# Fills in pieces, stores waited for later in attention, and two buffers of spread sums at the output stage

## The reference, cut to what matters

```python
def longformer_mask(n):           # allowed: |i - j| <= 64, or i == 0, or j == 0
    ...
def attention(x):                 # 8 batches, 16 heads of 16
    Q, K, V = (split_heads(x @ W + b) for W, b in ((Wq, bq), (Wk, bk), (Wv, bv)))
    p = softmax(einsum('bhqd,bhkd->bhqk', Q, K) * 0.25 + mask)
    return merge(einsum('bhqk,bhkd->bhqd', p, V)) @ Wo + bo
def ffn(h):                       # 4096 tokens, 16 experts, each takes its 512 best tokens
    scores = softmax(h @ gate_w.T).T
    w, idx = top_k(scores, 512)
    g, u = h[idx] @ Wg.T, h[idx] @ Wu.T
    out = zeros.at[idx].add((gelu(g) * u) @ Wd.T * w)
    return out + (gelu(h @ Sg.T) * (h @ Su.T)) @ Sd.T
x = x + attention(layernorm(x))
x = x + ffn(layernorm(x))
```

## Time and profile before

| what | us |
|---|---|
| median of 3 runs | 1283.11 |
| the profiled execution | 1284.79 |
| its span, first to last instruction | 1282.8 |
| TensorE busy | 1158.4 (90%) |
| VectorE, GpSimd, ScalarE busy | 854.4, 630.6, 597.9 |
| first transposes of TensorE | 28.4 |
| attention's first instruction | 117.8 |
| output stage's first load | 441.3 |
| experts' stage, first to last | 698 to 1282.8 |
| granted clock of TensorE, mean | 0.955 of full speed |

### The profile page before, as it was taken

How to read it: one execution, slowest core, us unless ns; L and a number is a source line. 1 busy time by engine, 2 the same in 40 slices (tenths; PEclk the granted TensorE clock), 3 DMA queues, 4 the chain that set the end, 5 groups by cost and what they waited for, 6 DMA issues and landing times. The chain is left out here.

```text
span 1282.8 us, 23570 instructions
## 1 busy us (share of the span) xinstructions
PE 1158.4 (90%) x8906; PEld 969.1 (76%) x8906; DVE 854.4 (67%) x2182; ACT 597.9 (47%) x961; POOL 630.6 (49%) x792
## 2 busy tenths in 40 slices
PE   0997799989999549999985999999999999999997
PEld 0885577766677349987874788888888888888886
DVE  7895677767777057747876766666677666766641
ACT  1341466656666425432222555545455555545442
POOL 8000356656565426411001476666666676677654
PEclk9997699989999868999997999999999999999999
DMA  2589477777775376210132444444444444444311
GB/s 92 183 292 133 151 119 126 129 128 131 129 122 97 90 189 191 66 54 34 35 114 80 150 120 111 132 106 109 132 129 125 125 104 127 103 127 127 92 29 17
DMA packets 63053, 149.08 MB, mean 116 GB/s; under 512 B 15168, under 2 KB 32064, under 8 KB 53728
## 3 DMA queue, kind: packets, MB, share of 16 engines
q1 hardware_dynamic: 50592, 130.71, 39.3%
q0 software_dynamic: 12352, 16.92, 7.8%
HBM read 104.73 MB, written 42.34 MB: 115 GB/s over the span
## 5 line engine op out<-in xcount | busy, mean ns | idle before, releaser
L611 DVE CUSTOM_DVE_ANT_0 junk_s<-ps_s,mask 128x258 bf16<-128x258 f32 (+2 forms) x512 | 212.6, 470 | 91.8 <-PE ps_s L692 91.0
L1852 POOL TENSOR_TENSOR held<-h,held 128x512 fp32r<-128x512 f32 x128 | 178.4, 1406 | 124.0 <-ACT held L1888 123.8
L665 ACT ACTIVATE pt<-ps_p 128x516 f32<-128x516 f32 (+2 forms) x256 | 167.1, 680 | 82.0 <-PE ps_p L713 67.6
L1962 PE MATMUL ps_gu<-xt_hi,w_hi 128*128 128x512 f32 x512 | 203.3, 397 | 2.1 <-DVE xt_lo L1911 2.1
L1962 PE MATMUL ps_gu<-xt_lo,w_hi 128*128 128x512 f32 x512 | 200.2, 391 | 0.0
L1962 PE MATMUL ps_gu<-xt_hi,w_lo 128*128 128x512 f32 x512 | 200.0, 391 | 0.0
L1927 DVE TENSOR_TENSOR h<-ge,ps_gu 128x512 f32<-128x512 f32 x128 | 87.9, 686 | 165.1 <-ACT ge L1882 141.1
L1790 DVE TENSOR_TENSOR w_lo<-w,w_hi 128x768 fp32r<-128x768 f32 x128 | 174.7, 1369 | 31.1 <-ACT w_hi L1785 27.6
L498 POOL TENSOR_SCALAR_AFFINE_SELECT pt<-pt 128x256 f32<-128x256 f32 x352 | 133.0, 417 | 119.8 <-ACT pt L665 119.6
L1979 PE MATMUL ps_y<-w_hi,held 128*128 128x256 f32 x1024 | 187.9, 282 | 3.4 <-ACT stage L1898 1.7
L692 PE MATMUL ps_s<-ks,qs 96*128 96x258 f32 (+2 forms) x512 | 157.3, 364 | 9.3 <-PEq L198 9.1
(11 more groups left out here) (198 smaller groups left out, 2140.5 us busy)
## 6 DMA issues: line engine op xcount, KB each, us to landing
w<-in_We SPq DMA_DIRECT2D x48, 1024.0 KB, 4.9
qk_parts<-held SPq DMA_DIRECT2D x8, 2064.0 KB, 7.8
qs<-qk_parts SPq DMA_DIRECT2D x96, 129.0 KB, 4.2
ks<-qk_parts SPq DMA_DIRECT2D x96, 129.0 KB, 5.6
x<-in_x SPq DMA_DIRECT2D x16, 512.0 KB, 7.9
attn_t<-on SPq DMA_DIRECT2D x32, 256.0 KB, 5.9
ot<-attn_t SPq DMA_DIRECT2D x16, 256.0 KB, 4.6
rd<-rden SPq DMA_DIRECT2D x16, 256.0 KB, 4.1
```

What stands on the lines that cost most here:

```text
L611: dve.tensor_tensor_reduce(junk[:, (u * SG + g) % RING, 0:n], ps_s[:, (u * SG + g) % RING, 0:n], m, 1.0, -3e38, ALU.add, ALU.max, mx[:, u ...
L665: act.activation(dst, src, ACT.Exp, scale=SCALE).then_inc(exp_s, 1)
L1852: pool.tensor_tensor(h_lo[:, m], h32[:, (e * KI + m) % HB], h_hi[:, m].bitcast(F32), ALU.subtract).then_inc(hlo_s, 1)
L1962: last = pe.matmul(ps_gu[:, m % 2, n], l, r, start=c == 0, stop=c == 3 * KD - 1)
```

## The change

1. Projection: instead of three memsets ahead of the loop, GpSimd fills one place of `qs` (zeros) and of `ks` (ones, all rows) at a time: place 0 first, places 1 to 4 in steps 1 to 4 behind a wait for `xn_s`. The casts of mask and identity move to step 5. SP waits for the ten memsets before it loads the places.
2. The store of projection's last batch is issued as attention's first DMA, behind the barrier.
3. Attention: `store_rden(b)` moves from step 3 of batch b+1 to step 0 of batch b+2 and no longer waits for its store; `load_den` waits for it instead. The wait at the end for attention's stores goes to the output stage, ahead of the load of the last sums.
4. ScalarE does `far_rows(u + 1)` behind the seventh exponential, ahead of `out_rows`, instead of behind the sixth.
5. Output stage: `rd` becomes two buffers (the second is the tile `xg`, not yet used). Loads go in the order rd 0, ot 0, x 0, rd 1, ot 1, x 1, wait for attention's stores, sums, x 2 and so on. The load of rd b waits for division b-2.

```diff
-                sp.wait_ge(ready, 4)
+                sp.wait_ge(fill_s, 2 * SL)
                 for u in range(SL):
                     sp.wait_ge(out_s[u // UB % 2], (u // UB // 2 + 1) * 16)
                     load_step(sp, d, ks, qs, qk_in, u)
                 step(B // 2 - 1, 0, False)
-                step(B // 2 - 1, 1, False)
...
-                pool.memset(qs[:].bitcast(F32), 0.0).then_inc(ready, 1)
-                pool.wait_ge(ready, 2)
-                pool.memset(ks[:].bitcast(F32), 0.0).then_inc(ready, 1)
-                pool.wait_ge(ready, 3)
-                pool.memset(ks[M_ROW:M_ROW + 2].bitcast(F32), 1.0).then_inc(ready, 1)
...
+                def fill(place):
+                    pool.memset(qs[:, place].bitcast(F32), 0.0).then_inc(fill_s, 1)
+                    pool.memset(ks[:, place].bitcast(F32), 1.0).then_inc(fill_s, 1)
+                fill(0)
                 for b in range(B):
+                    if 1 <= b < SL:
+                        pool.wait_ge(xn_s, b + 1)
+                        fill(b)
+                    if b == SL:
+                        pool.wait_ge(m_in, 16)
+                        pool.tensor_copy(mask[:], m32[:]).then_inc(ready, 1)
+                        pool.wait_ge(i_in, 16)
+                        pool.tensor_copy(ident16[:], ident[:]).then_inc(ready, 1)
                     pool.wait_ge(qlo_s, b * 4 + 4)
...
                     for s in range(2):
                         sp.wait_ge(out_s[s], 16 * (UB // 2) * (b + 1))
+                    if b >= 1:
+                        sp.wait_ge(rden_out, b * 16)
...
                 def store_rden(b):
                     sp.wait_ge(rden_s, b + 1)
                     sp.dma_start(d["rden"][b].rearrange("h (c i) -> (h c) i", i=DC), den[:]).then_inc(rden_out, 16)
-                    sp.wait_ge(rden_out, b * 16 + 16)
...
+                sp.dma_start(d["qk"][B - 1].rearrange("c (m t) d h q -> (t d h) c m q", m=KD),
+                             qk[:, 1].rearrange("p c m k i -> p c m (k i)").bitcast(F32)).then_inc(qk_out[1], 16)
                 m_rows(0)
...
-                    if b >= 1 and t == 3:
-                        store_rden(b - 1)
+                    if b >= 2 and t == 0:
+                        store_rden(b - 2)
+                store_rden(B - 2)
                 store(NU - 2)
                 store(NU - 1)
+                sp.wait_ge(rden_out, (B - 1) * 16)
                 sp.wait_ge(bo_in, 16)
-                for h in range(2):
-                    sp.wait_ge(out_s[h], 16 * NU // 2)
...
+                        if n == 6 and u + 1 < NU:
+                            far_rows(u + 1)
                         if n == 6 and u >= 1:
                             out_rows(u - 1)
-                        if n == 5 and u + 1 < NU:
-                            far_rows(u + 1)
...
-        rd = sb("rd", [P, KD, S])
+        rd = [sb("rd", [P, KD, S])[:], lists.xg[:].rearrange("p c n -> p (c n)").rearrange("p (k q) -> p k q", k=KD)]
...
                 def load_rd(b):
-                    if b >= 1:
-                        sp.wait_ge(on_s, b)
+                    if b >= 2:
+                        sp.wait_ge(on_s, b - 1)
...
+                load_rd(0)
                 load_ot(0)
-                load_rd(0)
                 load_x(0)
+                load_rd(1)
                 load_ot(1)
                 load_x(1)
+                for h in range(2):
+                    sp.wait_ge(ot_out[h], 16 * NU // 2)
                 den_rows = d["ot"][B - 1].rearrange("t (h r) (c i) -> t h r c i", r=32, i=DC)[:, :, DH]
                 sp.dma_start(den[:], den_rows).then_inc(den_in, 16)
-                load_rd(1)
...
-                    dve.wait_ge(rd_in, (b + 1) * 32)
-                    dve.tensor_tensor(ot[:, b % 2], ot[:, b % 2], rd[:], ALU.mult).then_inc(on_s, 1)
+                    dve.wait_ge(rd_in[b % 2], (b // 2 + 1) * 16 * KD)
+                    dve.tensor_tensor(ot[:, b % 2], ot[:, b % 2], rd[b % 2], ALU.mult).then_inc(on_s, 1)
```

More of the change, by code:

```diff
@@ L122, in build, with mlp @@
         qk_out = [sem("p_out0"), sem("p_out1")]
+        ot_out = [sem("a_out0"), sem("a_out1")]
         project(nc, d, sem, tally, ident, bias, eps, ks, qs, v, mask, ident16, qk_in, qk, qk_out)
-        attend(nc, d, sem, tally, ks, qs, v, mask, ident16, qk_in, qk_out, held, stage)
+        attend(nc, d, sem, tally, ks, qs, v, mask, ident16, qk_in, qk, qk_out, held, stage, ot_out)
         att.close()
-        mlp(nc, d, sem, tally, ident, eps, held, stage)
-def mlp(nc, d, sem, tally, ident, eps, held, stage):
+        mlp(nc, d, sem, tally, ident, eps, held, stage, ot_out)
+def mlp(nc, d, sem, tally, ident, eps, held, stage, ot_out):
     TT = T // P
@@ L147, in mlp @@
         weights = ExpertWeights(nc, ctx, sem)
-        front(nc, d, sem, tally, ident, eps, group, wparts, pm, probs, seg, cur, blk, before, lists, weights, ht_b, held, stage)
+        front(nc, d, sem, tally, ident, eps, group, wparts, pm, probs, seg, cur, blk, before, lists, weights, ht_b, held, stage, ot_out)
         weights.place_parts(nc, ctx)
@@ L180, in project @@
         whi = sem("p_whi")
+        fill_s = sem("p_fill")
         ready = sem("p_ready")
@@ L233, in _ @@
                 pool.memset(eps[:], EPS).then_inc(ready, 1)
-                pool.wait_ge(ready, 1)
-                pool.memset(qs[:].bitcast(F32), 0.0).then_inc(ready, 1)
-                pool.wait_ge(ready, 2)
-                pool.memset(ks[:].bitcast(F32), 0.0).then_inc(ready, 1)
-                pool.wait_ge(ready, 3)
-                pool.memset(ks[M_ROW:M_ROW + 2].bitcast(F32), 1.0).then_inc(ready, 1)
-                pool.wait_ge(ready, 4)
-                pool.wait_ge(m_in, 16)
-                pool.tensor_copy(mask[:], m32[:]).then_inc(ready, 1)
-                pool.wait_ge(i_in, 16)
-                pool.tensor_copy(ident16[:], ident[:]).then_inc(ready, 1)
-                pool.wait_ge(ready, 6)
-                for b in range(B):
+                def fill(place):
+                    pool.memset(qs[:, place].bitcast(F32), 0.0).then_inc(fill_s, 1)
+                    pool.memset(ks[:, place].bitcast(F32), 1.0).then_inc(fill_s, 1)
+                fill(0)
+                for b in range(B):
+                    if 1 <= b < SL:
[6 more added lines that the diff above has]
+                        pool.tensor_copy(ident16[:], ident[:]).then_inc(ready, 1)
                     pool.wait_ge(qlo_s, b * 4 + 4)
@@ L417, in load_step, with attend @@
             sp.dma_start(dst[n * DH:(n + 1) * DH, u % SL].bitcast(F32), d["qk"][u // UB, part, u % UB]).then_inc(qk_in[u % SL], 16)
-def attend(nc, d, sem, tally, ks, qs, vs, mask, ident16, qk_in, qk_out, held, stage):
+def attend(nc, d, sem, tally, ks, qs, vs, mask, ident16, qk_in, qk, qk_out, held, stage, out_s):
     with ExitStack() as ctx:
@@ L801, in _, with front @@
                     times_v(NU - 1, i)
-def front(nc, d, sem, tally, ident, eps, group, wparts, pm, probs, seg_probs, cur, blk, before, lists, weights, ht_b, held, stage):
+def front(nc, d, sem, tally, ident, eps, group, wparts, pm, probs, seg_probs, cur, blk, before, lists, weights, ht_b, held, stage, ot_out):
     UG = UB // KD
@@ L876, in front @@
         ot_in = [sem("o_ot_in0"), sem("o_ot_in1")]
-        rd_in = sem("o_rd_in")
+        rd_in = [sem("o_rd_in0"), sem("o_rd_in1")]
         x_in = [sem(f"o_x_in{b}") for b in range(B)]
@@ L951, in load_rd @@
                 def load_rd(b):
-                    if b >= 1:
-                        sp.wait_ge(on_s, b)
+                    if b >= 2:
+                        sp.wait_ge(on_s, b - 1)
                     for k in range(KD):
-                        sp.dma_start(rd[:, k], d["rden"][b, k * (NH // KD):(k + 1) * (NH // KD), :].unsqueeze(0)
-                                     .to_broadcast([DH, NH // KD, S])).then_inc(rd_in, 16)
+                        sp.dma_start(rd[b % 2][:, k], d["rden"][b, k * (NH // KD):(k + 1) * (NH // KD), :].unsqueeze(0)
+                                     .to_broadcast([DH, NH // KD, S])).then_inc(rd_in[b % 2], 16)
                 def load_x(b):
```

1 line of the change is left out of this document (removed).

## The result

The changed kernel takes 1251.85 us (median of 4 runs, 1250.91 to 1253.89), the kernel before 1282.51 beside it (4 runs, 1281.70 to 1285.75). The ratio is 0.9758, 95% interval 0.9737 to 0.9780: 2.4% faster. The forecast was 1251.6. The profiled execution took 1251.19, its span is 1249.5.

What follows compares the result with a forecast made beforehand. TensorE in the expert stage bounds the kernel, so gains only shift that stage's start. 19.1 + 0 + 10.7 + 1.7 = 31.5 us off 1284.79 gives 1253.3, less 1.7 to the median: 1251.6; range 1243.5 to 1261.

Steps and rivals of the forecast that it cites:

- Fills: Projection: with small memsets the first xn is no longer held and all later work moves 19.1 us earlier.
- Last projection store: Seam of projection and attention: attention starts about 7.9 us earlier, but the rows of maxima do not; gain 0.
- Attention: Attention's steps: stores waited for later remove 11.5 us of excess, less 0.8 for ScalarE's new order; gain 10.7 us.
- The removable part: Attention: 11.5 of the 12.1 us by which 29 steps exceed 29 x 8.88, leaving 0.6 for VectorE's reciprocals.
- The 0.5 for transfers still late: Attention: 0.5 us taken off the gain for transfers that would still come late.
- The swap: ScalarE copies the rows of maxima behind the seventh exponential, not the sixth: 0.3 us lost, upper bound 6.
- End of attention: SP no longer waits for the last stores before the barrier; the output stage's first load goes 1.7 us earlier.
- Output stage: Output stage: exchanged load order makes no difference and the second buffer gives 0; at most 2.1 us lost.
- A: Projection loop: the small memsets hold VectorE, four steps 3.5 us longer, 1265.6 us; chance 0.07.
- B: Attention: late transfers come from the queue, not SP's waits; its gain falls to about 1, 1261.3 us; chance 0.16.
- C: Seam of projection and attention: rows of maxima land early and the 7.9 us are gained, 1243.7 us; chance 0.10.
- D: Projection: memset time does not follow row length, ten take 8.7 us each; slower, 1296 us; chance 0.02.

Runs made afterwards that it cites:

- experiment 1: The kernel before with only the fills in pieces, nothing else of the change: 1264.27 us, ratio 0.9837.
- Experiment 2: The changed kernel with all ten small memsets back to back ahead of the projection loop: 1258.28 us, ratio 0.9796.
- experiment 5: The changed kernel with projection's last store back ahead of the barrier: 1252.67 us, ratio 0.9761.
- the repeated run: The changed kernel run again without an edit: 1252.23 us, ratio 0.9767.
- experiment 4: The changed kernel with ScalarE's copy of the rows of maxima back behind the sixth exponential: 1251.08 us, ratio 0.9752.
- experiment 3: The changed kernel with the reciprocal sums' store and SP's wait for it back at their old place: 1259.82 us, ratio 0.9804.
- experiment 8: The changed kernel with the wait for attention's last stores back at attention's end: 1254.86 us, ratio 0.9779.
- experiments 7: The changed kernel with three places loaded in projection, and step 0's rows of maxima ahead of place 3, the last store and place 4: 1240.97 us, ratio 0.9666.
- experiment 11: The changed kernel with rows of maxima ahead, their copy behind the sixth exponential, projection's last store in four parts over steps 1 to 4: 1235.01 us, ratio 0.9636.

## Why the prediction was right

The forecast of 1251.6 stands 0.3 from the measured median. The mechanisms were right, but that it is so near is in part luck. At the output stage's first load the traces show 31.8 us for the 31.5 of the sum, but with 1.0 more at the seam and 0.8 less from there on; another 1.3 came behind that load, where nothing was forecast. So the two profiled executions lie 33.6 us apart (1253.3 was forecast, 1251.19 measured), and the medians 30.7.

- **Fills, 19.1 predicted.** 19.2 to 19.3 at three stations, and experiment 1 alone moves the first exponents' arguments by 20.2. The reading behind it was right: the xn instructions had been held by the memsets, two of the four by a whole one, the first by the rest of one, and the last hardly (2.05, 8.86, 8.86 and 0.97 us). The estimate of 1.75 to 1.95 for a piece met 1.82, and the margin to the next xn was there (1.19 us at 36.72). Experiment 2 gives the price of ignoring it.
- **Last projection store, 0 predicted.** Right by experiment 5: attention started 7.8 us later, ScalarE got its rows within 0.1 us of the same time. The first exponents' arguments came 0.9 us earlier than the fills explain in this trace; experiments 1 and 5, which have the store at its old place, have that too (121.24, 121.40), and the repeated run has 0.2 only. So it is not the store's; what it is stays open.
- **Attention, 10.7 predicted, 10.4 found.** The removable part was 11.5. The 0.5 for transfers still late was not needed: none was late. The swap was mis-sized: I put 0.3 for it, argued that it fits with 0.1 to spare, and it costs 0.04 in each step, 29 x 0.04 = 1.2 by the steps and 0.99 by experiment 4. Step 30, outside the 29, is 0.37 longer as well (7.95 for 7.58). That SP's standing still at this store was the cause is shown by experiment 3, which gives back 8.5 of the 10.4 when it alone returns. But the prediction priced only the landing, 2.9 us each time, and passed over the 8.3 us that SP waited for the reciprocals at the same place; the change removes both. Of the remaining 1.9, experiment 1 has 1.65 with the fills alone; the rest may be hidden by the swap, which experiment 3 keeps.
- **End of attention, 1.7 predicted.** 1.66 between the two traces from TensorE's last product to the first load, 1.68 by experiment 8.
- **Output stage, 0 predicted for the order and the second buffer.** The second buffer was read rightly: the division it frees starts 2.7 us nearer to the first product, and ScalarE's instruction behind it does not move. The order stays open within 1 us.
- **The rivals.** A (pieces hold VectorE in the loop): xn keeps 1.38 beside all pieces. B (the queue's own lateness): refuted by the changed kernel, which has the same loads and no late step, and by experiment 3; the late steps go with SP's waits. C (the seam gives its 7.9): refuted by experiment 5, because the rows pass nothing in the queue. But its upper bound was too small as a bound for the seam: experiments 7 and 11 show that 16 us lay there, for an order of the queue that this change does not make. D (memset time not by row length): 1.82 for 2064 elements, 8.70 for 10320.

## What to carry to other kernels

Ask of each late small transfer what stands before it in its issuer's program and in its queue: SP stood still some 2.9 us for a landing nobody needed yet and up to 1.9 for a reciprocal, and that cost up to 5.5 us of TensorE in one place; four small copies taken out from behind a 2 MB store and twelve loads brought attention's first step 16.7 us forward. Starting a stage earlier brings nothing while its first real input still stands behind the same transfers; put the small transfer first and spread the bulk over the steps behind it. Cut long GpSimd fills into pieces and place them right behind the VectorE operation they would hold.

## What the runs showed of the hardware that I had not expected

The output stage, from its first product to the start of the expert stage, has the same instructions in all these kernels, and took between 242.6 and 249.8 us. The first 120 us of it, for the changed kernel, its repetition, and experiment 1 (columns as in the window above):

```profile
421.99:541.99 120.00, 106.49 (x674) 97.94 (x675) 74.41 (x165) 49.78 (x60) 46.92 (x26) 0.87 0.42 124
```

```profile
421.55:541.55 120.00, 106.29 (x670) 97.86 (x671) 73.55 (x164) 49.77 (x60) 46.95 (x26) 0.85 0.43 125
```

```profile
430.90:550.90 120.00, 103.27 (x640) 94.80 (x641) 72.43 (x161) 47.85 (x58) 47.76 (x26) 0.86 0.44 126
```

The stage took 242.7, 243.4 and 249.8 us in these three, and the mean granted clock of the first 120 us does not order them: 0.85 goes with 243.4 and 0.86 with 249.8. A shorter stretch does show part of it. The 14 us that begin 118 us behind the first product, for the changed kernel and for experiment 1:

```profile
539.99:553.99 14.00, 12.67 (x66) 10.86 (x67) 9.13 (x24) 5.20 (x7) 6.59 (x6) 0.88 0.11 39
```

```profile
548.90:562.90 14.00, 14.00 (x63) 12.71 (x62) 4.80 (x10) 4.42 (x5) 1.26 (x1) 0.63 0.11 37
```

In experiment 1 TensorE is busy for all of the 14 us at 0.63, in the changed kernel for 12.67 at 0.88; 14 x (0.88 - 0.63) = 3.5 us of full speed less, by this estimate half of the 7.1 by which the stage is longer. Experiment 2, with a stage of 248.7, also has 0.63 there, and the repetition 0.88. What decides it I can't say: I made no experiment on it. It is why one profile of a kernel is not enough to settle a difference of 2 us behind this stage, while the 29 steps of attention repeated to 0.01 us in the two profiles of the changed kernel.

Windows 106 to 121 us of the changed kernel and of experiment 11, at the seam:

```profile
106.00:121.00 15.00, 0.00 (x0) 0.00 (x0) 0.75 (x5) 0.00 (x0) 0.21 (x1) 0.50 0.90 294
```

```profile
106.00:121.00 15.00, 14.85 (x138) 10.99 (x137) 11.66 (x58) 9.86 (x16) 7.64 (x22) 0.90 0.65 97
```

In the changed kernel TensorE does nothing in these 15 us and its granted clock is at the lower level, 0.50, while the DMAs are 90% busy with the loads and stores that stand before four small copies. In experiment 11 the same microseconds hold nearly two steps of full work. The low clock adds nothing that can be seen: both kernels begin step 0 at it (0.55 over the first 4 us in the changed kernel, 0.50 in experiment 11), and step 0 takes 8.39 and 8.28 us.
